# Both direct groups first, an earlier weight comparison and 512-column projection matmuls in a modulated FFN

## The reference

```python
# _L0_cond_ref: v = x [16, 256, 512], q = cond_1024 [16, 256]
q_emb = jax.nn.relu(q @ W3 + b3)
n = v.shape[1]                                   # 256
v_sum = jnp.sum(v, axis=1, keepdims=True)
x = (n * v + v_sum) * q_emb[:, None, :]
return jax.nn.relu(x @ W2 + b2)
...
# _L0_ffn_ref: TH_X, SC_X = (0.33, 0.5), TH_W, SC_W = (0.2, 0.6)
x_q = ternary_quantize(x, TH_X, SC_X)
w_q = ternary_quantize(weight, TH_W, SC_W)
w_rram = w_q + rram_variation
return jnp.einsum('bsd,od->bso', x_q, w_rram)
...
x = x + _L0_ffn_ref(_L0_cond_ref(x, cond_1024, ...), weight, rram_variation)
```

## Time and profile before

| | |
|---|---|
| median of 3 runs | 198.66 us (198.41 to 199.66) |
| profiled execution: time | 198.73 us |
| profiled execution: span of the trace | 196.9 us |
| PE busy | 179.1 us (91%), 804 records |
| DVE busy | 114.9 us (58%) |
| ACT busy | 60.8 us (31%) |
| POOL busy | 23.2 us (12%) |
| DMA | 28.99 MB, mean 147 GB/s |
| chain that ended last, by engine | PE 68%, DVE 14%, SP queue 5%, DMA 4% |

### The profile page before, as it was taken

The page is one execution under the profiler, slowest core; times in us unless marked ns, Lnnn a source line. Parts: engine busy times, 40 slices in busy tenths (PEclk is TensorE's granted clock), DMA queues, the critical chain, the costliest instruction groups (busy, mean ns, idle before and its releaser), DMA issues.

```text
span 196.9 us, 2207 instructions
## 1 busy us (share of the span) xinstructions
PE 179.1 (91%) x804; PEld 133.9 (68%) x804; DVE 114.9 (58%) x133; ACT 60.8 (31%) x157; POOL 23.2 (12%) x26
## 2 busy tenths in 40 slices
PE   7989999496992099999999999999999999999994
PEld 2759995144450099886766878767668788988994
DVE  1847999687799614459975544499325322322333
ACT  2044445500099990202998202019400000000000
POOL 2004900004951900000000000000000000000000
PEclk9957999789999579999999999999999999999999
DMA  5999999999000999766112114911121137113124
GB/s 164 295 223 222 212 218 223 230 263 186 7 3 7 322 267 221 251 221 258 53 57 106 53 53 143 336 57 53 53 107 53 57 99 275 53 55 109 54 107 160
DMA packets 31002, 28.99 MB, mean 147 GB/s; under 512 B 1536, under 2 KB 22288, under 8 KB 30992
## 3 DMA queue, kind: packets, MB, share of 16 engines
q1 hardware_dynamic: 30320, 28.58, 55.1%
q10 hardware_dynamic: 608, 0.28, 0.6%
q0 software_dynamic: 64, 0.00, 0.0%
HBM read 20.47 MB, written 8.39 MB: 147 GB/s over the span
## 4 chain that ended last, share of the span: by engine, by line
PE 68%; DVE 14%; SPq 5%; DMA 4%; issue 3%; POOL 2%; ACT 2%; POOLq 1%; DVEq 0%
PE out_ps L674 31%; PE hid_ps L757 7%; DVE xT L363 6%; PE hid_ps L612 5%; PE hid_ps L648 4%; PE hid_ps L660 4%; PE hid_ps L627 4%; DMA x_in<-in_x 4%; PE hid_ps L605 4%; PE hid_ps L640 3%; PE hid_ps L667 3%; DVE x_sum L394 2%; SPq L195 2%; POOL wT_lo L287 2%; DVE wT L526 1%
## 5 line engine op out<-in xcount | busy, mean ns | idle before, releaser
L674 PE MATMUL out_ps<-wT_lo,hid 128*128 128x256 f32 x252 | 70.6, 319 | 8.3 <-POOL wT_lo L287 8.3
L674 PE MATMUL out_ps<-wT_hi,hid 128*128 128x256 f32 x252 | 62.3, 286 | 0.0
L674 PEld LDWEIGHTS out_ps<-wT_lo,hid 128*128 128x128 f32 x252 | 49.1, 195 | 12.4 <-POOL wT_lo L287 9.1
L674 PEld LDWEIGHTS out_ps<-wT_hi,hid 128*128 128x128 f32 x252 | 49.2, 195 | 4.8 <-issue 4.8
L481 DVE SCALAR_TENSOR_TENSOR x_res<-out_ps,x_res 128x512 f32<-128x512 f32 x31 | 21.3, 687 | 29.5 <-PE out_ps L674 29.5
L306 ACT ACTIVATE xT<-xT,coef,q_scale 128x256 f32<-128x256 f32 x64 | 33.2, 590 | 13.2 <-DVE coef L396 12.8
L363 DVE STREAM_TRANSPOSE xT<-x_in 128x1024 f32<-128x1024 f32 x15 | 30.6, 2047 | 3.8 <-DMA x_in<-in_x 3.8
L317 ACT ACTIVATE junk<-xT,q_emb 128x256 bf16<-128x256 f32 x40 | 19.8, 495 | 38.8 <-DVE xT L363 38.8
L612 PE MATMUL hid_ps<-xT,w_sb 128*128 128x512 f32 x24 | 13.0, 684 | 2.6 <-ACT e L327 2.6
L757 PE MATMUL hid_ps<-xT,w_sb 128*128 128x512 f32 x32 | 14.8, 606 | 0.0
L648 PE MATMUL hid_ps<-t_sum,s_mix 128*128 128x512 f32 x24 | 11.4, 595 | 1.6 <-DVE n L447 1.6
(11 more groups left out here) (64 smaller groups left out, 160.6 us busy)
## 6 DMA issues: line engine op xcount, KB each, us to landing
out<-x_res SPq DMA_DIRECT2D x31, 256.0 KB, 2.0
x_in<-in_x SPq DMA_DIRECT2D x28, 256.0 KB, 7.3
x_res<-in_x SPq DMA_DIRECT2D x3, 2048.0 KB, 8.4
x_res<-in_x SPq DMA_DIRECT2D x2, 1024.0 KB, 7.8
w_sb<-in_L_cond_W SPq DMA_DIRECT2D x4, 256.0 KB, 6.1
x_res<-in_L_ffn_weight SPq DMA_DIRECT2D x4, 256.0 KB, 7.0
x_res<-in_L_ffn_rram_variation SPq DMA_DIRECT2D x4, 256.0 KB, 7.0
w_sb<-in_L_cond_W SPq DMA_DIRECT2D x1, 512.0 KB, 4.2
```

The source lines that it names most:

```text
L674: mm = nc.tensor.matmul(bank[:, cols], hid[:, g % 2, k, c * P:(c + 1) * P], w[:, k, cols], start=(k == 0 and w is wT_lo), stop=(k == KD - ...
```

## The change

The split of the work is changed, not what is computed.

- The direct groups are batches 0 and 1, and 2 and 3; the super groups are batches 4 to 7, 8 to 11 and 12 to 15. The first two share one group of eight tiles. There is no direct group at the end.
- Pair 3 of x is loaded ahead of the weight, and the residual of eight tiles behind rram, ahead of pair 4.
- DVE compares the weight between the transposes of batches 6 and 7; batches 4 and 6 are summed by ACT, 5 and 7 by DVE. `token_sums_34` is split in two, with `sum_16` between them in the first super group.
- Each half of the weight's transpose waits for two quarters; the casts and the subtraction for `wT_lo` go by halves of the output columns, each behind its own transpose.
- The wait for `wT_lo` now stands ahead of tile 0 in the midst of the first super group (behind its second p7), and the tiles of the direct groups are projected between its last products.
- `project_part` covers 512 columns: eight matmuls per tile instead of 16. The last tile keeps two halves.
- Four matmuls on zeros are put between the parts of the `q_emb` product (three of them ahead of its semaphore), and the two behind it become five.
- POOL starts on `s_mix` when the coefficients of batch 3 are ready, not those of batch 1.

```diff
-    WARM, WARM_2 = 10, 2
+    WARM, WARM_2 = 10, 5
...
             load_pair(2)
+            sp.wait_ge(s_tr, 1)
+            load_pair(3)
             for q in range(QUADS):
                 sp.dma_start(w_in[q * BLK:(q + 1) * BLK], weight_split[q]).then_inc(s_w, DMA)
             for q in range(QUADS):
                 sp.dma_start(r_in[q * BLK:(q + 1) * BLK], rram_split[q]).then_inc(s_r, DMA)
-            sp.wait_ge(s_tr, 1)
-            load_pair(3)
+            load_res(0)
             sp.wait_ge(s_tr, 3)
             load_pair(4)
-            load_res(0)
...
-            pool.wait_ge(s_wT, 2)
-            for k in range(KD):
-                pool.wait_ge(s_whi, k + 1)
-                nc.gpsimd.tensor_tensor(wT_lo[:, k], wT[:, k], wT_hi[:, k].bitcast(F32), ALU.subtract).then_inc(s_wlo, 1)
+            for h, cols in enumerate(COLS):
+                pool.wait_ge(s_whi, h + 1)
+                nc.gpsimd.tensor_tensor(wT_lo[:, :, cols], wT[:, :, cols], wT_hi[:, :, cols].bitcast(F32),
+                                        ALU.subtract).then_inc(s_wlo, 1)
...
+            sum_and_scale(4)
+            scale_summed(5)
+            sum_and_scale(6)
             copy_p1(1, 0)
-            scale_summed(5)
+            scale_summed(7)
             copy_p1(1, 1)
...
+            quantize(0, 0)
+            quantize(0, 1)
+            quantize(0, 2)
+            quantize(0, 3)
+            transpose_batch(4)
             prepare(5)
-            quantize(FIRST, 3)
+            quantize(1, 0)
+            transpose_batch(6)
+            dve.wait_ge(s_w, QUADS * DMA)
+            nc.vector.tensor_scalar(w_gt, w_in, TH_W, SC_W, ALU.is_gt, ALU.mult).then_inc(s_wq, 1)
+            dve.wait_ge(s_wq, 1)
+            nc.vector.tensor_scalar(w_in, w_in, -TH_W, SC_W, ALU.is_lt, ALU.mult).then_inc(s_wq, 1)
+            quantize(1, 1)
+            prepare(7)
+            quantize(1, 2)
+            quantize(1, 3)
...
+            for m in range(KD):
+                pe.wait_ge(s_xs, 4 * KD)
+                pe.wait_ge(s_cls_hid, m + 1)
+                for k in range(KD):
+                    mm = nc.tensor.matmul(hid_ps[m][:], chunk_columns(w2_sb[:, k], m), xT[:, 0, k, TOK:],
+                                          start=(k == 0), stop=(k == KD - 1))
+                mm.then_inc(s_cls, 1)
...
             p7(1, 1)
+            project(0, 0)
+            project(0, 1)
+            project(0, 2)
             p4(1, 1)
+            project(0, 3)
+            project(0, 4)
+            project(0, 5)
             p3(1, 1)
-            pe.wait_ge(s_wlo, KD)
-            for c in range(4):
-                project(FIRST, c)
+            project(0, 6)
+            project(0, 7)
...
-                project_half(g, c, out_ps[i % 4], COLS[0])
-                project_half(g, c, out_ps[i % 4], COLS[1]).then_inc(s_out_ps, 1)
+                if i == 0:
+                    pe.wait_ge(s_wlo, 2)
+                project_part(g, c, out_ps[i % 4], slice(0, D)).then_inc(s_out_ps, 1)
```

More of the change, by code:

```diff
@@ L67, in adaln_ffn_kernel @@
     rram_split = rram.rearrange("(n t) (q f) -> q t n f", t=BLK, q=QUADS)
[L70 to L73, removed]
+    GROUPS = B // 4
+    LAST = GROUPS - 1
+    TILES = 8
+    VECTOR_SUMS = (0, 1, 2, 3, 5, 7)
+    SCALAR_SUMS = tuple(n for n in range(B) if n not in VECTOR_SUMS)
     ctx = ExitStack()
@@ L128, in adaln_ffn_kernel @@
         s_x_in = [sem(f"x_in_loaded{p}") for p in range(PAIRS)]
-        s_x_res = [sem(f"x_res_loaded{g}") for g in range(LAST + 1)]
-        s_stored = [sem(f"stored{g}") for g in range(LAST + 1)]
+        s_x_res = [sem(f"x_res_loaded{g}") for g in range(GROUPS)]
+        s_stored = [sem(f"stored{g}") for g in range(GROUPS)]
         s_cond_zero = sem("cond_zeroed")
@@ L178, in slot_of @@
         def slot_of(n):
[L180 to L187, removed]
+            return n // 4 % 2, slice(n % 4 * N, n % 4 * N + N)
         block = ctx.enter_context(nc.Block())
@@ L327, in copy_p1 @@
                 nc.scalar.activation(e1[:, j], hid_ps[j][:], ACT.Copy, scale=-1.0).then_inc(s_e1, 1)
-            for n in range(5):
+            for n in range(4):
                 scale_summed(n)
+            sum_and_scale(4)
+            scale_summed(5)
+            sum_and_scale(6)
             copy_p1(1, 0)
-            scale_summed(5)
+            scale_summed(7)
             copy_p1(1, 1)
[L334 to L345, removed]
+            for h, cols in enumerate(COLS):
+                act.wait_ge(s_wT, h + 1)
+                nc.scalar.copy(wT_hi[:, :, cols], wT[:, :, cols]).then_inc(s_whi, 1)
+            for n in range(8, 12):
+                sum_and_scale(n)
+            copy_p1(2, 0)
+            copy_p1(2, 1)
+            for n in range(12, 16):
+                sum_and_scale(n)
+            copy_p1(3, 0)
+            copy_p1(3, 1)
         @block.vector
@@ L391, in prepare @@
                 s, cols = slot_of(n)
+                done = VECTOR_SUMS.index(n)
                 transpose_batch(n)
@@ L394, in prepare, with quantize @@
                 nc.vector.tensor_reduce(x_sum[:], xT[:, s, :, cols], AX.X, ALU.add).then_inc(s_sum, 1)
-                dve.wait_ge(s_sum, n + 1)
+                dve.wait_ge(s_sum, done + 1)
                 nc.vector.tensor_tensor(coef[:, n], x_sum[:], q_emb[:, n], ALU.mult).then_inc(s_coef, 1)
[L398 to L404, removed]
+            def quantize(h, m):
+                dve.wait_ge(s_cls, KD * h + m + 1)
+                nc.vector.tensor_scalar(hid[:, 0, m, h * TOK:(h + 1) * TOK], hid_ps[m][:], b2_col[:, m:m + 1], TH_X,
                                         ALU.add, ALU.is_gt).then_inc(s_cls_hid, 1)
@@ L507, in _ @@
             c11(1, 1)
[L508 to L510 removed]
+            token_sum_3(1)
             sum_16(1, 0)
[L512 to L513 removed]
+            token_sum_4(1)
+            transpose_weight(0)
             sum_167(1, 0)
             c22(1, 0)
+            transpose_weight(1)
             c21(1, 0)
             sum_16(1, 1)
[L518 removed]
             c12(1, 0)
[L520 removed]
+            transpose_batch(8)
             sum_167(1, 1)
             c22(1, 1)
[L523 to L529 removed]
+            finish(0, 0)
+            transpose_batch(9)
+            finish(0, 1)
+            finish(0, 2)
+            c21(1, 1)
+            transpose_batch(10)
+            finish(0, 3)
+            finish(0, 4)
+            transpose_batch(11)
+            finish(0, 5)
             c12(1, 1)
[L531 to L534 removed]
+            finish(0, 6)
+            finish(0, 7)
             for g in (2, 3):
@@ L549, in _ @@
                 c21(g, 0)
-                if g == 2:
-                    transpose_batch(4 * g + 4)
+                if g < LAST:
+                    transpose_batch(4 * g + 6)
                 sum_16(g, 1)
@@ L587, in _ @@
                                           start=(k == 0), stop=(k == KC - 1))
-            mm.then_inc(s_q_ps, 1)
+                if m == KD - 1:
+                    mm.then_inc(s_q_ps, 1)
+                nc.tensor.matmul(out_ps[3][:], warm[:, 0:P], warm[:], start=True, stop=True)
             for _ in range(WARM_2):
```

156 lines of the change are left out of this document (58 added, 98 removed).

## The result

The changed kernel takes 179.75 us (178.53 to 180.84, four runs), beside 198.55 us for the kernel before on the same chip: ratio 0.904, 95% interval 0.897 to 0.911. That is 18.8 us, about 9.5%, less. The prediction was 176.4 us with a range of 174.8 to 181.0. The profiled execution took 179.71 us, with a span of 177.9.

A forecast was written before the change was run, and what follows sets the result against it. PE was taken to bound the kernel, with waits and half-clock stretches before tile 0. Waits 13.2, half clock 3.1, tiles 5.7, start 0.9, less 0.8, gave 22.1; 22.3 was taken: 198.7 to 176.4 us, range 174.8 to 181.0.

The forecast's parts named there:

- the three waits of 13.2 us: PE idle ahead of the projection, for ACT's copy of p1, DVE's `n16` and `wT_lo`; all three were to go, 13.2 us.
- margins that don't hold: Four places in the DVE and ACT chain with 0.2 to 0.4 us to spare; 0.8 us allowed (0 to 2).
- the walk: Step-by-step times for DVE, ACT, POOL and DMA, set against when PE wants each product, up to tile 0 at 63.3.
- token sums at 1.14 from 47.0: DVE's token sums in the first super group: 1.14 us each from 47.0, the second done at 49.3, wanted at 49.6.
- PE's idle time up to tile 0 under 1 us: Sign that the forecast holds: PE waits less than 1 us in all before the first projection tile.
- The half clock: Two later half-clock stretches of PE, behind gaps without work, were to go: 1.6 and 1.5 us, 3.1 together.
- 512-column projection: 31 tiles in eight matmuls of 512 columns: 1.73 us a tile (up to 1.81), gain 5.7 us (3.3 at the other bound).
- a tile is not under 1.81: Sign of being wrong: a projection tile of 512-column matmuls takes 1.81 us or more, where 1.73 was expected.
- The start: Added matmuls on zeros bring the full clock sooner; first direct group ends at 28.3, gain 0.9 us (-0.7 to +1.0).
- The wait for `wT_lo` only moves: Rival: DVE slips, PE stands 2.5 us more for `wT_lo` and loses 1.5 to the clock; 180.5 us, chance 0.12.
- 512 columns cost what twice 256 do: Rival on the projection: 240 ns per 512-column matmul, 5.7 us less gain, 182.1 us; chance 0.07.
- The remaining three: Rivals: later super groups wait, 179 us (0.05); float32r at float32 rate, near 336 (0.01); matmuls at 131 ns, 155 (0.01).

## Why the prediction was right, and where it was off

- **The waits.** Right: the three waits of 13.2 us went. Left over is one of 2.0 us; the prediction allowed 0.8 (0 to 2) for margins that don't hold. Its cause was not such a margin: the walk priced the token sums at 1.14 from a stretch in which POOL did nothing, and moved them beside POOL's additions, where they took 2.26 and 2.17. That is the step that failed, "token sums at 1.14 from 47.0", and so "PE's idle time up to tile 0 under 1 us" didn't hold. The additions behind the sums (178.17 us) and the earlier comparison (178.43) show it. Of the thin margins one did fail in seven traces, that of the second copy of p1 (0.2 us to spare by the walk): PE is held 0.4 us, and its chain, too, goes through an operation beside POOL, batch 7's coefficients. In the changed kernel's trace it costs 0.1.
- **The half clock.** Right: no stretch behind 17 us, so the 3.1 us that the prediction priced for the two went, and a pause of 2.0 us brought none.
- **512-column projection.** The mechanism is right, the size was off. The term was 5.7 us for tiles of 1.73; the trace has 1.83 to 1.86, outside even my upper bound of 1.81, and the tiles gave 31 x (1.91 - 1.83) = 2.5. The prediction named "a tile is not under 1.81" as a sign of being wrong, and it came true. I took float32 `s_mix` matmuls as the nearest row for a float32r matmul because width and layout agreed. The type was what counted: bfloat16 runs at 216 ns, float32r at 227 to 232, at 256 columns 109 and 120. The row of the same type at the other width was nearer: its 13.2 ns over the columns give 226.5.
- **Not seen:** pairs p1 and p2 and the direct group became cheaper, 3.43 for 3.54, some 0.5 to 0.9 us.
- **The start.** The forecast was 28.3 for the end of the first direct group, and it ended near 27.8 here. As a claim on the zeros it isn't borne out: without them the time is the same. When the clock rises differs between executions, and what an early rise gains is cut off by ACT's scaling of batch 3. That this trace beat the forecast is in part luck.
- **The sum.** PE's end was put at 171.8 and is 175.31. By parts: p6 could have begun 0.5 earlier than forecast (49.1), then 1.2 more of wait than allowed and 0.3 until PE is back in step, which makes tile 0 start at 65.1 and not 64.1; then from tile 0 to the end 110.2 against 107.7, of which the tiles are +3.1 and the cheaper products -0.7. Forecast and time differ by 3.35 us, inside the range. The two steps above (projection 3.1 us too cheap, wait 1.2) were each off the same way; the earlier p6 and the cheaper products, neither of them foreseen, made up for 1.2 of it.
- **Rivals.** "The wait for `wT_lo` only moves" did not come; what came is a wait for another product of the same DVE and POOL stretch. With the comparison left late, PE waits ahead of p3, since the weight's transpose holds up DVE's list. "512 columns cost what twice 256 do" was nearer to the truth than I gave it credit for: 230 ns against 240, where I expected 217. The remaining three show nowhere.

## What to carry to other kernels

When a step is moved so that it runs beside another engine's work, price it from a row with the same neighbour, not from one where that engine was idle: here DVE's sums of two SBUF operands cost up to almost double beside GpSimd's additions, and a product on 128x4 elements took 1.14 us for 0.16. For a matmul that no row shows, the type was here a nearer likeness than the width. And a weight's preparation spread over four engines belongs where each engine's in-order list is idle, since the piece that waits holds up all that is queued behind it, which is how a late comparison stopped a product that doesn't need the weight.

## What the runs showed of the hardware

- A float32r matmul costs 13 ns over its columns at 256 and 14 to 19 at 512 (119.9; 1.83 to 1.86 us for eight), a bfloat16 one under 3 at both (109; 216).
- float32 products with strided weights (p1, p2) run 3.43 to 3.45 us a pair between tiles of 512-column matmuls and 3.54 or 3.55 between tiles of 256, whatever the type of the tiles.
- A DVE sum of two 128x1024 operands in SBUF took 1.2 us alone and up to 2.26 beside GpSimd's additions, whose four took 4.94 to 4.99 us alone and 5.92 to 6.94 beside the sums. A product on 128x4 elements took 0.16 us alone and up to 1.14 beside GpSimd's subtractions.
- The granted clock came back to full between 12.4 and 15.6 us in seven traces with the same matmuls on zeros at the start, and three more show it at 1.00 throughout although their zeros ran at the half level's pace, so a single trace says little about such a start.
